# A perceiver layer on one core: the first projections of self-attention are interleaved with the last tile of cross attention

## The reference

```python
def cross(h, ctx):                       # h = layernorm(x)
    Sim  = h @ w1 + (ctx @ w2).T + (h * w3) @ ctx.T + b_sim
    hq   = softmax(Sim, over ctx) @ ctx
    hc   = softmax(max(Sim, over ctx), over tokens) @ h      # one row per batch
    return concat([h, hq, h * hq, h * hc]) @ W_qv + b_qv
x = x + cross(layernorm(x), ctx_1024)
x = x + self_attention(layernorm(x))     # 16 heads of 32, causal; q, k, v, Wm
x = x + ffn(layernorm(x))                # shared experts, and 2 of 8 routed
```

## Time and profile before

| | us |
|---|---|
| median of 3 runs | 1434.79 (1433.67 to 1434.84) |
| the profiled execution | 1433.62 |
| its span in the trace | 1431.9 |
| first matmul of tile 15's `attend` | 591.30 |
| `attend(15)` ends, PE idle until 612.55 | 606.12 |
| `project` of tiles 2 and 3 begins | 659.30 |
| mean granted PE clock, share of full speed | 0.984 |

### The profile page before, as it was taken

The page is one execution under the profiler, slowest core; times in us unless marked ns, Lnnn a source line. Parts: engine busy times, 40 slices in busy tenths (PEclk is TensorE's granted clock), DMA queues, the critical chain, the costliest instruction groups (busy, mean ns, idle before and its releaser), DMA issues.

```text
span 1431.9 us, 20806 instructions
## 1 busy us (share of the span) xinstructions
PE 1368.9 (96%) x7264; PEld 808.1 (56%) x7265; DVE 678.1 (47%) x1251; ACT 303.3 (21%) x518; POOL 167.6 (12%) x197
## 2 busy tenths in 40 slices
PE   6988999999999999979999999999999999999996
PEld 2333444444444444358888887899884444444573
DVE  3234455544444444457777776675432222222244
ACT  2011111111111111125333334323221111111110
POOL 0100000000000000111311003004310000000065
PEclk9999999999999999989999999999999999999998
DMA  9999999999999999526000001314373322222176
GB/s 367 396 400 400 396 391 395 388 384 365 367 361 363 370 363 361 183 87 266 2 0 0 0 0 60 139 69 176 120 274 91 111 92 84 93 74 73 52 230 189
DMA packets 101534, 305.40 MB, mean 213 GB/s; under 512 B 10065, under 2 KB 30545, under 8 KB 101489
## 3 DMA queue, kind: packets, MB, share of 16 engines
q1 hardware_dynamic: 96368, 288.01, 53.7%
q0 software_dynamic: 5120, 16.78, 3.6%
HBM read 269.62 MB, written 35.13 MB: 213 GB/s over the span
## 4 chain that ended last, share of the span: by engine, by line
PE 46%; DVE 3%; issue 3%; POOL 2%; DMA 2%; ACT 1%; SPq 0%; POOLq 0%; DVEq 0%; ACTq 0%
PE ps L1735 11%; PE ps L2013 9%; PE ps L2000 9%; PE ps L1725 8%; PE ps L1551 3%; PE ps L1771 2%; POOL arena L571 2%; DMA arena<-w2t 1%; PE ps L1754 1%; PE ps L1743 1%; PE ps L1864 1%; POOL idx L567 1%; ACT arena L585 0%; DMA moe_in<-arena,idx 0%; PE ps L1613 0%
## 5 line engine op out<-in xcount | busy, mean ns | idle before, releaser
L585 ACT ACTIVATE arena<-ps 128x512 f32<-128x512 f32 x155 | 90.6, 597 | 608.0 <-PE ps L1551 311.8
L1652 PE MATMUL ps<-arena 128*64 128x512 f32 (+1 forms) x832 | 192.0, 597 | 0.0
L1590 PE MATMUL ps<-arena 128*64 128x512 f32 (+1 forms) x1024 | 179.9, 506 | 4.2 <-DVE arena L921 2.9
L1735 PE MATMUL ps<-split 128*128 128x256 f32 x1344 | 171.1, 287 | 1.2 <-DVE split L1092 1.2
L1735 PEld LDWEIGHTS ps<-split 128*128 128x128 f32 x1344 | 165.1, 193 | 6.4 <-issue 5.6
L997 DVE SCALAR_TENSOR_TENSOR arena<-arena,hbar 128x512 f32<-128x512 f32 x128 | 91.9, 759 | 109.3 <-PE ps L1613 105.2
L2013 PE MATMUL ps<-arena 128*128 x312 | 140.4, 592 | 1.2 <-DMA arena<-w2t 1.2
L2000 PE MATMUL ps<-arena 128*128 x312 | 140.4, 593 | 0.4 <-DVE arena L1375 0.4
L1590 PEld LDWEIGHTS ps<-arena 128*64 128x64 f32 x1024 | 66.2, 138 | 130.3 <-issue 122.6
L1652 PEld LDWEIGHTS ps<-arena 128*64 128x64 f32 (+1 forms) x832 | 58.6, 138 | 113.6 <-issue 113.2
L2013 PEld LDWEIGHTS ps<-arena 128*128 128x128 f32 x312 | 59.0, 190 | 75.2 <-issue 75.2
(11 more groups left out here) (175 smaller groups left out, 1549.9 us busy)
## 6 DMA issues: line engine op xcount, KB each, us to landing
arena<-ctx_t SPq DMA_DIRECT2D x128, 800.5 KB, 13.7
arena<-ctx_n SPq DMA_DIRECT2D x128, 768.0 KB, 9.2
moe_in<-arena SPq DMA_DIRECT2D x3, 3328.0 KB, 24.0
arena<-moe_in SPq DMA_DIRECT2D x156, 64.0 KB, 1.9
moe_out<-arena SPq DMA_DIRECT2D x39, 256.0 KB, 2.1
arena<-w1t SPq DMA_DIRECT2D x1, 7168.0 KB, 23.1
arena<-ctx_n SPq DMA_DIRECT2D x32, 130.0 KB
arena<-w2t SPq DMA_DIRECT2D x4, 1024.0 KB
```

What stands on the lines that cost most here:

```text
L585: return nc.scalar.activation(o, i, ACT.Copy)
L1590: last = mm(bank(n)[S * h:S * (h + 1), 0:w], qT[:, k, S * h:S * (h + 1)], ctxT[h][:, k, at_j:at_j + w], start=(k == 0), stop=(k == KD - 1))
L1652: last = mm(bank(7)[S * h:S * (h + 1), :], ET[0:w, c, S * h:S * (h + 1)], ctxN[h][0:w, c, :], start=(c == 0), stop=(c == JC - 1))
L1735: last = mm(dst[:, 2 * P * m:2 * P * (m + 1)], w[a][:, k, c], tokens[b][:, k, :], start=(k + i == 0), stop=(k == KD - 1 and i == 2))
```

## The change

It moves instructions in each engine's order and lays the buffers out anew; none is added to the computation.

- `h1T` moves down to where the context's transposed copy was, so it is free before `attend(15)`; `Kbd` and `Vbd` move up; tiles 0 and 1 are normed into `hc` and into the buffer of `qT`, and transposed to banks 4 and 0.
- `finish_norm(4, ...)` covers tiles 0 to 13 and stands before `maxima(15)`; its square root stands before `exp_scores(15)` on ACT. Tile 14 goes to `finish_norm(5, ...)`.
- PE transposes tiles 0 and 1 between `exp_T(15)` and `attend(15)`. A new `start_b` puts the rest of tile 15's cross attention between the first query, key and value projections.
- `Kbd[1]` is cleared after `feats_done` rather than before it, and `wait_ge(vbd_zero, 2)` moves behind tile 15's residual.
- The first weight has a semaphore of its own (`wq_in`), and POOL waits for `v_done` of the last tile before it splits ws1.

```diff
--- before.py
+++ after.py
...
         w_lo = [as_split(carve(KD, D)) for _ in range(4)]
+        h1T = [as_split(carve(KD, 2 * P)) for _ in range(2)]
+        w_hi = [as_split(carve(KD, D)) for _ in range(4)]
+        attnT = [[as_split(carve(KD, P)) for _ in range(2)] for _ in range(2)]
         h1 = [carve(D) for _ in range(2)]
-        w_hi = [as_split(carve(KD, D)) for _ in range(4)]
-        h1T = [as_split(carve(KD, 2 * P)) for _ in range(2)]
-        attnT = [[as_split(carve(KD, P)) for _ in range(2)] for _ in range(2)]
+        h1_0 = [hc, qT.rearrange("p k n -> p (k n)")]
         assert used[0] == SPLIT, used[0]
-        Kbd = [carve(KD, 2, HG * S) for _ in range(2)]
-        assert used[0] <= 2 * KD * J + 2 * JC * D, used[0]
-        Vbd = [carve(2, H // 2, 2 * HD) for _ in range(2)]
         qhT = carve(KD, 2 * P)
         khT = carve(KD, 2 * P)
+        Kbd = [carve(KD, 2, HG * S) for _ in range(2)]
+        assert used[0] - 2 * KD * HG * S <= 2 * KD * J + 2 * JC * D, used[0]
+        Vbd = [carve(2, H // 2, 2 * HD) for _ in range(2)]
         sm = carve(H, S)
...
+        def h1T_bank(i, first):
+            return bank(4 if first and i == 0 else 0 if first else i)
         def logits(g):
...
         ctxN_in = [sem(f"ctxN_in{q}") for q in range(NP)]
-        attnw_in = sem("attnw_in")
+        wq_in, attnw_in = sem("wq_in"), sem("attnw_in")
         rows_in = sem("rows_in")
...
             sp.wait_ge(sim_done, KD * (T))
-            for dst, src in zip(w_raw, (wq, wk, wv, wm)):
-                sp.dma_start(dst, src.rearrange("(k p) n -> p k n", p=P)).then_inc(attnw_in, 16)
+            for i, src in enumerate((wq, wk, wv, wm)):
+                sp.dma_start(w_raw[i], src.rearrange("(k p) n -> p k n", p=P)).then_inc(wq_in if i == 0 else attnw_in, 16)
             sp.wait_ge(c_ready, T)
...
             pool.wait_ge(pv_done, NP * (T))
-            for i in range(2):
-                nc.gpsimd.memset(Kbd[i], 0.0).then_inc(kbd_zero, 1)
+            nc.gpsimd.memset(Kbd[0], 0.0).then_inc(kbd_zero, 1)
             pool.wait_ge(feats_done, T)
+            nc.gpsimd.memset(Kbd[1], 0.0).then_inc(kbd_zero, 1)
             for i in range(2):
...
             pool.wait_ge(ws1_in, 16)
+            pool.wait_ge(v_done, T)
             halves = [w.rearrange("p k (a n) -> p (k a) n", a=2) for w in (ws1_lo, ws1_hi, raw_ws1)]
...
             stage_a(T - 2, 0)
-            stage_a(T - 1, 1, more=False)
+            attended_copy(T - 2)
+            sqrt_of_var(4, 0, T - 2)
+            exp_scores(T - 1, False)
+            after_scores(T - 1, 1, more=False)
             def round_weights(i):
-                act.wait_ge(attnw_in, 64)
+                if i == 0:
+                    act.wait_ge(wq_in, 16)
+                else:
+                    act.wait_ge(attnw_in, 48)
                 nc.scalar.activation(w_hi[i], w_raw[i], ACT.Copy).then_inc(w_hi_ready, 1)
-            sqrt_of_var(4, 0, T - 1)
-            attended_copy(T - 1)
-            round_weights(0)
-            act.wait_ge(pv_done, NP * T)
...
                 nc.scalar.activation(h1T[0][:, :, P * i:P * (i + 1)],
-                                     bank(i).rearrange("p (k n) -> p k n", n=P), ACT.Copy).then_inc(h1hi_ready, 1)
+                                     h1T_bank(i, n is None).rearrange("p (k n) -> p k n", n=P), ACT.Copy
+                                     ).then_inc(h1hi_ready, 1)
...
                     keys(a, 0, n, first)
+                    if first:
+                        act.wait_ge(kbd_zero, 2)
                     keys(a + 1, 1, n, first)
...
             h1_high(1, 1, None)
+            round_weights(0)
+            act.wait_ge(pv_done, NP * T)
+            attended_copy(T - 1)
             for i in range(1, 4):
                 round_weights(i)
-            act.wait_ge(kbd_zero, 2)
+            act.wait_ge(kbd_zero, 1)
             stage_b(0, True, False, first=True)
-            sqrt_of_var(5, T - 1, T)
+            sqrt_of_var(5, T - 2, T)
             stage_b(1, True, True, second=True)
...
             stage_a(T - 2, 0)
-            stage_a(T - 1, 1, more=False)
...
                     dve.wait_ge(h1T_done, t - 1)
-                normed(h1[i], t).then_inc(h1_ready, 1)
+                normed(h1_0[i] if first else h1[i], t).then_inc(h1_ready, 1)
...
                 c = slice(P * i, P * (i + 1))
-                low_part(h1T[1][:, :, c], bank(i), h1T[0][:, :, c]).then_inc(h1lo_ready, 1)
+                low_part(h1T[1][:, :, c], h1T_bank(i, isinstance(t, int) and t < 2), h1T[0][:, :, c]
+                         ).then_inc(h1lo_ready, 1)
...
-            finish_norm(4, 2 * T - 1, 0, T - 1)
-            for i in range(2):
-                norm_b(i, i, True)
+            finish_norm(4, 2 * T - 2, 0, T - 2)
+            dve.wait_ge(hcT_done, T)
+            dve.wait_ge(hc2_ready, T)
+            norm_b(0, 0, True)
+            maxima(T - 1, False)
+            features(T - 2, 0)
+            norm_b(1, 1, True)
+            combined(T - 2, 0)
+            batch_max(T - 1, False)
+            exp_copies(T - 1, False)
+            batch_weights(T - 1, False)
+            combined(T - 2, 1)
+            h1_low(0, 0)
+            combined(T - 2, 2)
+            h1_low(1, 1)
+            combined(T - 2, 3)
+            low_weights(0)
+            residual_a(T - 2)
             attended(T - 1, False)
-            features(T - 1, (T - 1) % 2)
-            combined(T - 1, 0)
-            low_weights(0)
-            other_chunks(T - 1)
-            for i in range(2):
-                h1_low(i, i)
-            low_weights(1)
-            residual_a(T - 1)
             dve.wait_ge(rows_in, 64)
-            dve.wait_ge(vbd_zero, 2)
...
                 row_stats(t).then_inc(stats_ready, 1)
+            def start_b():
+                queries_b(0, 0, True)
+                features(T - 1, (T - 1) % 2)
+                low_weights(1)
+                queries_b(0, 1, True)
+                combined(T - 1, 0)
+                low_weights(2)
+                combined(T - 1, 1)
+                keys_b(0, 0, True)
+                combined(T - 1, 2)
+                keys_b(0, 1, True)
+                combined(T - 1, 3)
+                norm_b(2, 0)
+                norm_b(3, 1)
+                residual_a(T - 1)
+                dve.wait_ge(vbd_zero, 2)
+                values(0, 0, True)
+                masked_scores(0, True)
+                values(1, 1, True)
+                h1_low(2, 0)
+                h1_low(3, 1)
...
                     queries_b(n, 1, first)
-                if first:
-                    low_weights(2)
                 if last:
...
-            stage_b(0, True, False, first=True)
-            finish_norm(5, 2 * T, T - 1, T)
+            start_b()
+            finish_norm(5, 2 * T, T - 2, T)
             stage_b(1, True, True, second=True)
...
-            def normed_T_b(t, i):
+            def normed_T_b(t, i, first=False):
                 pe.wait_ge(h1_ready, t + 1)
-                transposes(bank(i), h1[i]).then_inc(h1T_done, 1)
+                transposes(h1T_bank(i, first), h1_0[i] if first else h1[i]).then_inc(h1T_done, 1)
...
                     normed_T(t + 1, False)
+                else:
+                    pe.wait_ge(F1_ready, T)
+                    normed_T_b(0, 0, first=True)
+                    pe.wait_ge(et_act, 2 * t + 1)
+                    normed_T_b(1, 1, first=True)
                 attend(t, i)
...
             stage_a(T - 1, 1, more=False)
-            attended_T(T - 1, False)
-            batch_means(T - 1)
-            for i in range(2):
-                normed_T_b(i, i)
-            features(T - 1)
-            for k in range(KD):
-                combined_chunk(T - 1, 1, k)
...
                     pe.wait_ge(h1lo_ready, a + 2)
-                    if first:
-                        pe.wait_ge(w_lo_ready, 1)
                     project(bank(1), wq_p, 0, h1T).then_inc(q_done, 1)
...
                     pe.wait_ge(q_ready, 2 * n + 1)
-                    if first:
-                        pe.wait_ge(w_lo_ready, 2)
                     project(bank(1), wk_p, 0, h1T).then_inc(k_done, 1)
...
                 if now:
-                    if not first:
-                        pe.wait_ge(vbd_ready, 4 * a)
-                    else:
-                        pe.wait_ge(w_lo_ready, 3)
+                    pe.wait_ge(vbd_ready, 4 * a)
                     project_v(0)
...
-            stage_b(0, True, False, first=True)
+            def start_b():
+                pe.wait_ge(h1hi_ready, 2)
+                pe.wait_ge(h1lo_ready, 2)
+                pe.wait_ge(w_lo_ready, 1)
+                project(bank(1), wq_p, 0, h1T).then_inc(q_done, 1)
+                attended_T(T - 1)
+                batch_means(T - 1)
+                project(bank(2), wq_p, 1, h1T).then_inc(q_done, 1)
+                features(T - 1)
+                combined_chunk(T - 1, 1, 0)
+                pe.wait_ge(q_ready, 1)
```

(19 more changed lines are left out.)

## The result

| | before | changed |
|---|---|---|
| median of 5 runs, us | 1434.62 | 1426.36 (1424.44 to 1428.35) |
| ratio, 95% interval | 1 | 0.9945 (0.9931 to 0.996) |
| profiled execution, us | 1433.62 | 1426.36 |
| distance D, us | 78.04 | 70.60 |

What follows compares the result with a forecast made beforehand. PE, waiting on DVE around tile 15's attention, was taken as the bound. Gain 10.5 less 1.7 and 1.0 for clock gave 7.8 us: 1433.62 to 1425.8, plus 1.17 for the median, 1427.0; range 1423.4 to 1431.0.

Steps and rivals of the forecast that it cites:

- Part 1: Norms before maxima(15): maxima start 3.9 us later, F3 comes late, new PE idle of 2.5 us in features(14).
- The table load: Sqrt load before exp_scores(15): 1.28 us; with the skill page's drain, idle 3.9 instead of 2.5; drain rival 1428.3, chance 0.05.
- Parts 2 and 3: Transposes before attend(15), then start_b: 0.9 us of PE moved earlier, low_weights(0) hidden, no PE idle for 28 us from 609.5.
- Part 4: Clearing of Kbd[1] and Vbd until 640.0 delays the values: 2.8 us idle before V1, later 1.9; gain 10.5 us.
- Part 5: Half clock after new idles: 1.7 us lost behind that in features(14), 1.0 behind that before V1; bounds 0 and 3.6.
- the rival without any loss: Gaps of 2.5 and 2.8 us keep full clock, as idles of 1.5 did: 10.5 us gained, 1424.3; chance 0.13.
- Part 6: POOL's b_m beside the mask of tile 0: 0 to 0.9 us, hidden; ws1 split starts later, about 883.5, also hidden.
- the main case: The whole kernel: likeliest 1427.0 us, spanning 1423.4 to 1429.5 with the bounds of clock and ports; chance 0.57.
- the six chances: Main case 0.57, no clock loss 0.13, more DVE-bound 0.14, table-load drain 0.05, gain given back 0.08, slower 0.03.
- The signs: Expected: features(14) idle, attend(15) then L1735 without idle, V1 waiting 2.8 us, projections at 650 to 652, later distances unchanged.
- the 18 us: Ceiling on the gain between 606.12 and 659.30: 12.9 us of PE idle and 5.2 of half clock and matmuls without successor.

Runs made afterwards that it cites:

- F3 first: Changed kernel with the maxima of tile 15 and F3 of tile 14 moved ahead of DVE's wait for the square root: 1420.88 us, ratio 0.9918.
- one experiment: Changed kernel with useless PE work in its two idles (two features(14) matmuls issued twice, scores of tile 0 computed twice): 1425.67 us, ratio 0.9952.
- the interleaved kernel with both its orders mended: Changed kernel with F3 before the square root and Vbd[0] cleared first: 1421.03 us, then 1418.87 against the changed kernel's 1425.38 on one chip.

## Why the prediction was right

- **Part 1, idle for F3:** 2.5 forecast, 2.22 measured; the maxima start 4.0 later against the start of D, forecast 3.9; the diagonal took 0.29, forecast 0.35.
- **The table load:** the root starts 0.01 us behind its load and the next load 0.02 behind the root (584.06 + 1.28, 585.35 + 0.21). The further drain of 1.38 us that the Trainium skill names ("ScalarE: Activation LUTs", What ACT_TABLE_LOAD costs) does not appear here; with it the prediction's estimate of the idle was 3.9. The advice of the same page of the Trainium skill ("Table sets: the hidden batching unit") is to do all exps together and then all sqrts. The change goes against it, but the loads were not what cost: with F3 first both loads stay and the idle is gone.
- **Parts 2 and 3:** `attend(15)` was followed by Q0 at once. From Q0 to the scores 28.3 us, forecast 27.6: a chunk between projections costs 1.01 by the distance of starts and not 0.87 (626.72 to 627.73), 0.6 for the four. This is the term that was mis-sized.
- **Part 4:** 2.64 of idle, forecast 2.8, released by L1169 behind the clearing. Last idle 1.41, forecast 1.9 at full clock and about 1 with the clock's part.
- **Part 5, clock:** 1.8 behind the first idle and 1.6 on V1, of which the last idle absorbed part; forecast 1.7 and 1.0 net. Here I was right for a weaker reason than I gave, and in part by luck. I went by seven idles of 2 to 4 us that were all followed by half clock; with 2.89 this held in one experiment, with 2.78 it failed in the three profiles that have it, and 1.86 did it in one kernel and not in the next. It is a likelihood, and the rival without any loss deserved more than 0.13. That rival's ground, that idles of 1.5 keep full speed, was wrong for the drain of the kernel before itself, where the third idle of 1.52 is followed by half clock (1.97 for 1.08, and 13.44 for 11.76):

```profile
631.61 1.97 PE L1613 MATMUL ps<-arena 128*64 128x512 f32 x4 [1.52 <-DVE arena L997]
633.51 13.44 PE L1735 MATMUL ps<-split 128*128 128x256 f32 x96
```

- **Part 6:** L1182, the subtraction, took 2.13 beside POOL, and V1's delay hid it. The later ws1 split cost nothing, which the run with that wait alone shows within its interval and by the 43.4 us.
- **Sum:** D fell by 7.44, forecast 7.8. The missing 0.4 is the 0.7 of Part 3 less some 0.3 by which the idles and the half clock together came out smaller. That the median still came within 0.6 us of 1427.0 is the scatter outside D. Two slips did not matter: the main case with its bounds ends at 1427.0 + 0.9 + 0.9 = 1428.8, not 1429.5, and the six chances add up to 1 already, which leaves no 0.09 for the unseen.
- **The signs:** F3's idle, Q0 behind `attend(15)`, V1 behind the clearing and the clock all came as said. The projections of tiles 2 and 3 start at 653.35, outside the 650 to 652 that was given; D starts 1.5 later in this profile, and counted from there it is 651.9. "All distances as before" from there on missed by the 0.5 us told above.
- **What the prediction did not ask:** how much of the 18 us a smaller edit would have taken. Its own first paragraph names L975 behind residual, norms and root as the releaser of 6.43; moving it ahead of them, with F3, ScalarE's copy and two transposes, gives 6.7.

## What to carry to other kernels

Where an engine in order holds up another, first look at what stands ahead of the awaited instruction and is needed later: moving it behind is cheaper than filling the idle with other work, and here it was worth nearly as much (D 71.36 against 70.60). Then add cover for the idles that are left: the interleaved kernel with both its orders mended reached 63.85. When independent work is used as cover, count the waits that come with it (here a root before the maxima, a clearing in the wrong order); they took 2.2 and 2.6 us of idle and 1.8 and 1.6 in clock. Compare small changes by a distance inside the trace between two fixed instructions, since the times of one kernel spread over 1 to 8 us where D repeated to 0.02, in two pairs of profiles.

## What the runs showed of the hardware

- Half clock after a short idle is not a matter of its length alone. The idle of 2.2 us in `features(14)` was followed by it in all four profiles that have it; 1.86 us was in one kernel and was not in another that differs only some 20 us earlier; 2.89 us was and 2.78 us was not. Of three idles of 1.52 us in a row the third was followed by it in every kernel with the four chunks in a row, and in one the second too. What decides between these was not tried. Behind a single idle of 1.7 to 2.9 us it cost 1.4 to 1.8 us.
- With 3.6 us of useless work in its idles PE finished D 1.8 us earlier, because the work kept the clock up; half clock behind another idle then took 1.4 back.
- Beside POOL's b_m additions of 1.25 us, DVE instructions of 0.15 us took 1.23, each until the addition beside it had ended. Delaying POOL moved this cost and didn't remove it. The Trainium skill ("GPSIMD Engine Reference", Key points) names this contention for DVE instructions with two SBUF inputs or in a 2-port perf mode. L880 and the subtraction have two SBUF inputs; L881, which took 1.23 too, has one, and in which mode it ran no trace shows.
